# A graph network on one core: destination rows centred by the matrix engine, and several small pieces of work put into other stages

## The chip, the cores and the metric

One core of a Trainium2 chip. The metric is device microseconds of one execution, and lower is better. The engines are PE (matrix), DVE (vector), ACT (scalar functions), POOL (GpSimd, which here issues the gathers and scatters by index) and SP, which only issues DMAs and clears semaphores. Each has its own instruction queue, and they meet only through semaphores.

## The reference

N = 50,000 nodes with 64 features, E = 25,000 edges sorted by destination `dst`; `src` is random. `_L0` is a graph attention network of four layers with four heads, `_L1` a convolution over edges with batch norm.

```python
h = relu(layernorm(x))
for l in range(4):                          # _L0, each edge and a loop of each node
    fs = (h @ Ws[l]).reshape(N, 4, 64)
    e = leaky_relu(el[src] + er[dst], 0.2)  # el, er: fs times attn_l, attn_r
    alpha = softmax of e over the edges that end in one node
    h = (segment_sum(alpha * fs[src], dst) + bias).sum(heads)
x = x + h + h_bias
h = relu(layernorm(x))
total = concat([h[src], h[dst], edge_attr]) @ W_full + b_full
filter, core = split(batch_norm(total), 2)
update = segment_sum(sigmoid(filter) * softplus(core), dst)
x = x + softplus(h + batch_norm(update))
```

## The kernel before

Edges lie in 196 tiles of 128, and one turn of a loop handles a group of 4 tiles (512 edges), so that each stage over edges has G = 49 turns. Since edges are sorted by destination, a segment sum is a running sum over 512 edges of a row (a scan on DVE) that a `keep` bit resets at a segment's start. `keep_row` holds these bits in DRAM.

The program is a row of stages with a barrier of all engines between them. Within a stage each engine's program is written by `pipelined(eng, stages, down, lead, slots)`: for turn i it calls each `(lag, fn)` in the order of the list, with group i − lag. The order within a turn, and so the order of the engine's queue, is that of the list; a greater lag sets a step later, and the stage runs G + lead turns. Group k's buffers are guarded by `wait_ge(signal, at(k, back=n))`. The stages and where they lie in the profiled execution, in us:

- Weights, 0 to 62.
- The first stage over edges, 62 to 568.6: POOL gathers the x rows of source and destination (L190), DVE and ACT layernorm both (`center`, `variance`, `normalize`), and PE makes projections and searches each edge's source among the destinations. The raw destination rows are stored in DRAM as `x_dst`.
- A short block of preparation, L1106 to L1173, 568.6 to 591.1. SP loads 28 pieces of `keep_row` (L1125). DVE turns the search's results into the row numbers `row_of_source` and `row_of_x1` (L1137 to L1151, 128 x 196 elements each), then makes the gate tables `keep`, `stop`, `open_f`, `reach`, `carry_in` out of the bits (L1154 to L1166, two scans of 896 among them). PE fetches four columns (L1173).
- Four layers, each of `softmax_weights`, `messages` and (but for the last) `spread`. A layer ends with `clear_signals`, a block of its own in which SP clears each semaphore in turn (L135).
- The last stage over edges, 2319.3 to 2641.6, groups in falling order, with LEAD = 8. Per group: POOL gathers x1 of the sources out of the message table (L1229). PE spreads the layer's result (L1269), DVE ends and scans it (L1313, L1320), ACT adds a constant (L1396, `h_full`), and PE transposes `h_full` into rows (`to_edges`, L1276). DVE centres the source rows (`center`: L1337 the sum, L1338 the subtraction), adds the destination's raw rows `x_again` to PE's rows (L1343, writing x1 into `edge`), and centres those too (L1346, L1348). Then ACT squares, DVE sums (L1353) and normalizes (L1358), PE transposes `norm` (L1283) and the edge attributes (L1291), multiplies both with the convolution's weights (L1297, L1298), and DVE takes the batch statistics (`bn_stats`, L1365).
- The conv stage, 2643.9 to 2953.7: ACT computes softplus and sigmoid (`norm1` L1505 and L1506, `exponential` L1511, `logarithm` L1515, `sigmoid` L1520), DVE multiplies (`message`, L1545), scans, ends and counts, PE transposes the sums into rows (`to_rows`), ACT copies them (`take_updates`, L1526), SP fetches x1 out of `edge` beside them (`load_x1`, L1472), and POOL scatters the rows to their nodes (L1488).
- The output over all nodes, 2955.4 to 3186.6, which begins with a memset of 128 x 8192 on DVE (L1687) that SP's loads wait for (L1640).

## Time and profile before

| | us |
|---|---|
| median of 3 runs | 3179.8 (3177.26 to 3186.66) |
| the profiled execution, its own time | 3188.4 |
| its span in the trace | 3186.6 |
| PE busy, of the span | 2305.1 (72%) |
| DVE busy | 2230.3 (70%) |
| POOL busy | 1434.1 (45%) |
| ACT busy | 1248.8 (39%) |

The shares are averages over stages with different limits, and none of them tells alone what the kernel is bound by: that is read stage by stage. Times in the rows below are us from the start of the span. A row such as `x4` with one duration is a run of like instructions, from the first start to the last end. An f32 matmul is recorded as two.

### The profile page before, as it was taken

The numbers are of one execution on the slowest core, as the hardware profiler recorded it, in microseconds if no ns is written. First come the engines' busy times: TensorE is split into PE (matmuls) and PEld (weight loads), VectorE is DVE, ScalarE is ACT, GpSimd is POOL, SyncE is SP. The second block draws the span as 40 slices with busy tenths as digits, with TensorE's granted clock in tenths as the row PEclk, the third lists the DMA queues.
The fourth block names the chain that finished last, engine by engine and source line by source line (L and its number), as shares of the span: only waits on it lengthen the run. The fifth ranks groups of instructions, "written<-read, shape, count | busy, mean of one in ns | idle before, by whom it ended". The sixth has DMA issues, their size and how long they took to land. (4 is left out here: it accounts for less than half of the span.)

```text
span 3186.6 us, 38276 instructions
## 1 busy us (share of the span) xinstructions
PE 2305.1 (72%) x10796; PEld 1490.8 (47%) x10796; DVE 2230.3 (70%) x3891; ACT 1248.8 (39%) x2599; POOL 1434.1 (45%) x1389
## 2 busy tenths in 40 slices
PE   1998888399899399898569898749967781110575
PEld 1766665255575255566345565425533330000564
DVE  4766665677776567687377687468889976664698
ACT  0332332144332144343134333124445547662586
POOL 5777775000577300377500177700067754777000
PEclk9999999999855599777589877569989975555898
DMA  2333333011453111254101155202233321222464
GB/s 60 105 102 101 100 96 84 13 47 46 105 125 87 16 37 46 70 143 113 25 23 46 52 133 134 41 20 79 79 74 71 73 55 35 65 72 64 146 199 141
DMA packets 310382, 248.80 MB, mean 78 GB/s; under 512 B 149840, under 2 KB 258639, under 8 KB 310154
## 3 DMA queue, kind: packets, MB, share of 16 engines
q1 hardware_dynamic: 266270, 197.56, 20.6%
q0 software_dynamic: 43904, 48.80, 8.7%
q8 instruction: 90, 1.47, 0.2%
q14 instruction: 118, 0.97, 0.1%
HBM read 125.76 MB, written 118.06 MB: 77 GB/s over the span
## 5 line engine op out<-in xcount | busy, mean ns | idle before, releaser
L933 POOL DMA_INDIRECT edge<-table,row_of_source x588 | 596.9, 1015 | 909.4 <-POOLq L753 731.2
L871 PE MATMUL banks<-scaled_t,w_heads 128*64 128x512 f32 x784 | 380.1, 607 | 0.0
L815 DVE TENSOR_TENSOR_SCAN wide<-keep,wide,banks 64x512 f32<-64x512 uint8 x196 | 249.5, 1273 | 185.9 <-issue 161.3
L1229 POOL DMA_INDIRECT edge<-table,row_of_x x196 | 226.3, 1155 | 305.9 <-POOLq L131 244.6
L849 ACT ACTIVATE ring<-wide 128x512 f32<-128x512 f32 x196 | 123.6, 630 | 425.4 <-DVE wide L815 425.4
L1073 ACT ACTIVATE wide<-h_new 64x512 f32<-64x512 f32 x147 | 92.6, 630 | 474.1 <-DVE h_new L1019 474.1
L981 PEld LDWEIGHTS banks<-w_edge_full,wide 128*128 128x128 f32 x1176 | 219.6, 278 | 122.7 <-issue 105.9
L1488 POOL DMA_INDIRECT node_rows<-rows_conv,scatter_row x196 | 218.9, 1117 | 118.8 <-ACT rows_conv L1526 68.2
L981 PE MATMUL banks<-w_edge_full,wide 128*128 128x72 f32 x1176 | 227.7, 360 | 54.9 <-DVE self_logit L1029 54.0
L878 PEld LDWEIGHTS banks<-w_row,ring 128*128 128x128 f32 x1568 | 190.4, 191 | 161.1 <-issue 149.3
L974 PE MATMUL banks<-wide,w_row 128*64 128x512 f32 x294 | 241.6, 920 | 19.4 <-DVEq L1006 10.1
L808 DVE TENSOR_TENSOR scaled<-edge,alpha 128x1024 f32<-128x1024 f32 x196 | 236.7, 1209 | 3.7 <-PE banks L863 3.7
L190 POOL DMA_INDIRECT edge<-in_x_dram,src_row x196 | 194.5, 992 | 81.7 <-issue 58.2
L190 POOL DMA_INDIRECT got<-in_x_dram,dst_row x196 | 194.5, 992 | 59.7 <-issue 59.7
L878 PE MATMUL banks<-w_row,ring 128*128 128x68 f32 (+1 forms) x1568 | 217.9, 282 | 4.7 <-ACT ring L849 4.7
L863 PE MATMUL banks<-ident,scaled 128*128 128x128 f32 x1568 | 210.4, 279 | 11.8 <-DVE scaled L808 11.8
L1602 PE MATMUL banks<-ident,last_sum 64*128 64x64 f32 x196 | 32.2, 318 | 248.3 <-ACT rows_conv L1526 192.7
L587 PE MATMUL banks<-w_chain,norm_t 64*128 64x204 f32 x392 | 204.7, 624 | 2.5 <-ACT self_logit L565 2.5
L863 PEld LDWEIGHTS banks<-ident,scaled 128*128 128x128 f32 x1568 | 184.0, 150 | 16.7 <-DVE scaled L808 13.3
L1019 DVE TENSOR_TENSOR_SCAN h_new<-keep_next,h_new,ended 64x512 f32<-64x512 uint8 x147 | 187.1, 1273 | 1.8
L996 PE MATMUL banks<-w_node,n_norm_t 65*128 65x64 f32 x784 | 136.9, 332 | 37.7 <-ACT n_norm_t L1089 37.7
L871 PEld LDWEIGHTS banks<-scaled_t,w_heads 128*64 128x64 f32 x784 | 91.7, 137 | 148.6 <-issue 148.3
(300 smaller groups left out, 4571.9 us busy)
## 6 DMA issues: line engine op xcount, KB each, us to landing
node_rows<-x_out SPq DMA_DIRECT2D x97, 256.0 KB, 2.6
wide<-node_rows SPq DMA_DIRECT2D x48, 512.0 KB, 3.6
table<-chain_rows SPq DMA_DIRECT2D x147, 136.0 KB, 2.2
table<-rows SPq DMA_DIRECT2D x147, 136.0 KB, 2.3
nodes<-in_x_dram SPq DMA_DIRECT2D x97, 128.0 KB, 2.5
table<-x_out SPq DMA_DIRECT2D x97, 128.0 KB, 2.4
out_dram<-n_soft SPq DMA_DIRECT2D x48, 256.0 KB, 2.1
sources<-src_pad SPq DMA_DIRECT2D x49, 196.0 KB
```

The lines of the kernel that those rows point to most:

```text
L190: pool.indirect_dma_start(out=to, out_offset=None, in_=x, in_offset=bass.IndirectOffsetOnAxis(ap=rows[:, tile:tile + 1], axis=0),).then_in ...
L587: t_.matmul(bank[4 + t // 2][:, (t % 2) * width:(t % 2 + 1) * width], mine[0:D], w_chain[:].rearrange("p l w -> p (l w)"), start=True, sto ...
L808: v.tensor_tensor(scaled[:, s], edge[:, tiles, 0:D].unsqueeze(2).broadcast_to([P, TPG, H, D]), inner(alpha[:, tiles], [P, TPG, H, D]), ALU ...
L815: v.tensor_tensor_scan(out=wide[0:D, bass.ds(g * GE + 1, GE)], data0=keep[:, s], data1=bank[2 + s][0:D], initial=wide[0:D, bass.ds(g * GE, ...
L863: last = t_.transpose(bank[6 * s + pair][:, t * P:(t + 1) * P], scaled[:, s, t, 2 * pair:2 * pair + 2].rearrange("p h f -> p (h f)"), iden ...
L871: last = t_.matmul(bank[2 + s][0:D], w_heads[:, l, pair], scaled_t[:, s, pair], start=pair == 0, stop=pair == 1)
L878: last = t_.matmul(bank[4 + s][:, t * width:(t + 1) * width], ring[:, s, t * P:(t + 1) * P], w_row[:, l, 0:width], start=True, stop=True)
L933: pool.indirect_dma_start(out=edge[:, at_tile], out_offset=None, in_=tables[l], in_offset=bass.IndirectOffsetOnAxis(ap=row_of_source[:, at ...
L974: t_.matmul(bank[s % 2][0:D], w_row[:, l, 0:D], wide[:, bass.ds(g * GE + 1, GE)], start=True, stop=True).then_inc(through, 1)
L981: last = t_.matmul(bank[2 + s % 2][:, t * EDGE_W:(t + 1) * EDGE_W], here, w_edge_full[:, l + 1], start=True, stop=True)
L1229: pool.indirect_dma_start(out=edge[:, tile, 0:D], out_offset=None, in_=tables[l], in_offset=bass.IndirectOffsetOnAxis(ap=row_of_x1[:, tile ...
L1488: pool.indirect_dma_start(out=node_rows, out_offset=bass.IndirectOffsetOnAxis(ap=scatter_row[:, tile:tile + 1], axis=0), in_=rows[:, s, t] ...
```

## The change

- **The last stage.** The first stage also stores the *centred* destination rows, as `x_mid` (`save_mid`). In the last stage PE adds them up itself: it multiplies `x_mid`'s rows (256 columns) with the identity, and each tile of `h_full` with `center_of` = identity − 1/64 in place of the transpose, all into one bank. ACT copies that bank into `norm` (`take_mid`, new), and DVE's L1343, L1346 and L1348 are gone. The four transposes of the attributes become two of 128 x 128, and the product with `attr_t` becomes two of 256 columns each, with weights padded by zeros.
- **The conv stage.** `x1` comes from the message table in DRAM. The lags shrink, `lead` goes from 7 to 3, and ACT's `take_updates` is the last step of its turn.
- **The block of preparation is gone.** The 28 loads and the gate tables move into turns 2 to 34 of the first stage. The row numbers (17 instructions) go to POOL, in `messages` of layer 0.
- **Clears.** The block of `clear_signals` becomes a list of retired semaphores, which SP clears inside the next `softmax_weights`. After the last stage and the conv stage nothing is cleared.
- In `softmax_weights` the memset of `chain` (L656) now stands behind the wait for ACT's logits. The memset of the output stage is gone.

```diff
@@ first stage @@
+                def save_mid(k, g, s, turn):
+                    sp.wait_ge(centered, at(k))
+                    sp.sem_inc(sp_paced, 1)
+                    sp.dma_start(x_mid.rearrange("p (t f) -> p t f", f=D)[:, bass.ds(k * TPG, TPG)], norm[:, s % 2, :, 1]).then_inc(mid_saved[s % 2], 16)
...
+                def load_gates(k, g, s, turn):
+                    if 0 <= k - LOADS_FROM < CH:
+                        c = k - LOADS_FROM
+                        sp.dma_start(keep_u[c * H:(c + 1) * H], lanes(keep_row[c * CE:(c + 1) * CE + 1], H)).then_inc(gates_in, 16)
...
-                pipelined(sp, ((1, save_x), (4, save), (0, load)), slots=SLOTS)
+                pipelined(sp, ((0, load_gates), (2, save_mid), (1, save_x), (4, save), (0, load)), slots=SLOTS)
...
+                    v.wait_ge(mid_saved[h], 16 * (k // 2 + 1))
...
-                pipelined(v, ((3, normalize), (2, variance), (2, look_up), (1, center), (1, reach)), slots=SLOTS)
+                pipelined(v, ((3, normalize), (2, variance), (2, look_up), (1, center), (1, mark_reached), (1, gate_tables)), slots=SLOTS)
@@ softmax_weights @@
+                @block.sync
+                def _(sp):
+                    clear_retired(sp)
...
+                    v.wait_ge(logit_ready, 4)
                     for n, start in enumerate((-BIG, 0.0)):
                         link(v.memset(chain[:, n], start))
-                    v.wait_ge(logit_ready, 4)
@@ last stage, PE @@
                 def to_edges(k, g, s, turn):
+                    t_.wait_ge(x_in[s], turn * 16 + 16)
+                    t_.wait_ge(mid_taken, at(k, back=1))
+                    t_.sem_inc(pe_paced, 1)
+                    t_.matmul(bank[2][:, 0:TPG * D], ident[:], x_again[:, s].rearrange("p t f -> p (t f)"), start=True, stop=False)
                     t_.wait_ge(full_ready, at(k))
-                    t_.wait_ge(x_used, at(k, back=1))
-                    t_.sem_inc(pe_paced, 1)
                     for t in range(TPG):
-                        last = t_.transpose(bank[2][:, t * D:(t + 1) * D], h_full[:, s, t * P:(t + 1) * P], ident[0:D, 0:D])
+                        last = t_.matmul(bank[2][:, t * D:(t + 1) * D], h_full[:, s, t * P:(t + 1) * P], center_of[:], start=False, stop=t == TPG - 1)
                     last.then_inc(full_t, 1)
...
-                    t_.matmul(bank[5 + s][:], w_conv3[:], attr_t[:], start=False, stop=True).then_inc(conv_ready, 1)
+                    for b in range(2):
+                        last = t_.matmul(bank[5 + s].rearrange("p (a b q) -> p b a q", b=2, q=P)[:, b], w_conv3[:, b], attr_t[:],
+                                         start=False, stop=b == 1)
+                    last.then_inc(conv_ready, 1)
@@ last stage, SP, DVE and ACT @@
-                    sp.wait_ge(x_used, at(k, back=2))
+                    sp.wait_ge(full_t, at(k, back=2))
...
-                    v.tensor_tensor(here, bank[2][:, 0:TPG * D].rearrange("p (t f) -> p t f", f=D), x_again[:, s], ALU.add).then_inc(x_used, 1)
...
-                    link(v.tensor_reduce(now[:, 0, :, 1], here, AX_X, ALU.add))
...
+                def take_mid(k, g, s, turn):
+                    s_.wait_ge(full_t, at(k))
+                    s_.wait_ge(norm_in_psum, at(k, back=2))
+                    s_.activation(norm[:, s, :, 1], bank[2][:, 0:TPG * D].rearrange("p (t f) -> p t f", f=D), ACT.Copy).then_inc(mid_taken, 1)
...
-                pipelined(s_, ((1, finish), (4, rstd), (3, squares), (5, take), (6, keep_conv)), down=True, lead=LEAD)
+                pipelined(s_, ((1, finish), (4, rstd), (3, take_mid), (3, squares), (5, take), (6, keep_conv)), down=True, lead=LEAD)
@@ conv stage @@
-                    sp.dma_start(rows[:, s, :, 0:D], edge[:, bass.ds(g * TPG, TPG), 0:D]).then_inc(x1_in[s], 16)
-
-                pipelined(sp, ((1, load), (4, load_x1)), lead=7, slots=SLOTS)
+                    sp.dma_start(rows[:, s, :, 0:D],
+                                 tables[L - 1][N:N + EP].rearrange("(p t) w -> p t w", p=P)[:, bass.ds(g * TPG, TPG)]).then_inc(x1_in[s], 16)
+
+                pipelined(sp, ((0, load), (0, load_x1)), lead=3, slots=SLOTS)
...
-                pipelined(s_, ((1, exponential), (2, logarithm), (3, sigmoid), (0, norm1), (6, take_updates)), lead=7, slots=SLOTS)
+                pipelined(s_, ((0, norm1), (1, sigmoid), (0, exponential), (0, logarithm), (2, take_updates)), lead=3, slots=SLOTS)
...
-                pipelined(v, ((5, end), (4, message), (2, larger), (4, scan), (5, count_in)), lead=7, slots=SLOTS)
+                pipelined(v, ((1, message), (1, scan), (0, larger), (1, end), (1, count_in)), lead=3, slots=SLOTS)
...
-                pipelined(t_, ((5, to_rows),), lead=7, slots=SLOTS)
+                pipelined(t_, ((1, to_rows),), lead=3, slots=SLOTS)
@@ output stage @@
-                sp.wait_ge(nodes_cleared, 1)
...
-                v.memset(nodes[:], 0.0).then_inc(nodes_cleared, 1)
```

PE's queue in the middle of the last stage, one turn of the kernel before:

```order
L1269 MATMUL banks<-wide,w_row 64x512
L1283 MATMUL banks<-ident,norm_last 128x128 x4
L1291 MATMUL banks<-ident,attr 64x128 x4
L1297 MATMUL banks<-norm_t_last,w_conv 128x512
L1298 MATMUL banks<-attr_t,w_conv 128x512
L1276 MATMUL banks<-ident,h_full_last 128x64 x4
```

The same turn of the changed kernel:

```order
L1303 MATMUL banks<-wide,w_row 64x512
L1319 MATMUL banks<-ident,norm_last 128x128 x4
L1327 MATMUL banks<-ident,attr 128x128 x2
L1333 MATMUL banks<-norm_t_last,w_conv 128x512
L1335 MATMUL banks<-attr_t,w_conv 128x2x128 x2
L1309 MATMUL banks<-x_last,ident 128x256
L1312 MATMUL banks<-center_of,h_full_last 128x64 x4
```

Two transposes of the attributes have gone, one product of 256 columns has come, and the product with the attributes and the four small steps at the end have other forms.

ACT's queue in the middle of the conv stage, one turn of the kernel before (`arg` and `soft` at the head are `norm1`, `rows_conv` is `take_updates`, `gate` is `sigmoid`):

```order
L1505 ACTIVATE arg<-wide,bn_scale 128x512
L1506 ACTIVATE soft<-wide,bn_scale 128x512
L1526 ACTIVATE rows_conv<-banks 128x4x64
L1511 ACTIVATE soft<-soft 128x512
L1515 ACTIVATE soft<-soft 128x512
L1520 ACTIVATE gate<-soft 64x512
```

The same turn of the changed kernel:

```order
L1533 ACTIVATE arg<-wide,bn_scale 128x512
L1534 ACTIVATE soft<-wide,bn_scale 128x512
L1548 ACTIVATE gate<-soft 64x512
L1539 ACTIVATE soft<-soft 128x512
L1543 ACTIVATE soft<-soft 128x512
L1554 ACTIVATE rows_conv<-banks 128x4x64
```

The copy of the rows has moved from the third place to the last, and its group is now two behind the turn's newest, where it was six behind.

## Rows read from the trace of the kernel before

**Rows 1.** Windows: stretch, length, busy us of PE, PEld, DVE, ACT, POOL, PEclk, DMA
```profile
625.00:817.00 192.00, 187.38 (x980) 110.31 (x980) 134.29 (x148) 80.00 (x148) 0.00 (x0) 0.99 0.13 45
2400.00:2500.00 100.00, 79.11 (x307) 35.07 (x306) 95.03 (x168) 55.42 (x119) 77.75 (x68) 0.95 0.33 73
2608.00:2644.00 36.00, 23.70 (x47) 9.53 (x46) 11.57 (x23) 9.85 (x22) 0.00 (x0) 0.50 0.03 7
```

**Rows 2.** Last stage, POOL's gathers: count with shortest/median/longest ns, first and last start
```profile
L1229 POOL DMA_INDIRECT edge<-table,row_of_x x196: 940/1120/1581, 2320.0 to 2606.7; - x196
```

**Rows 3.** Last stage, timeline of one turn, DVE and POOL; columns: start, duration
```profile
2455.00 1.28 DVE L1320 TENSOR_TENSOR_SCAN h_new_last<-keep_last,h_new_last,ended_last 64x512 f32<-64x512 uint8 x1
...
2455.55 1.49 POOL L1229 DMA_INDIRECT edge<-table,row_of_x  x1 [0.30 <-issue]
...
2457.68 0.42 DVE L1343 TENSOR_TENSOR edge<-banks,x_last 128x256 f32<-128x256 f32 x1
...
2459.04 0.69 DVE L1365 BATCH_NORM_STATS2 conv_stat<-banks 128x6 f32<-128x512 f32 x1
```

**Rows 4.** PE in that turn of the last stage, and one row of `messages`
```profile
2454.95 0.63 PE L1283 MATMUL banks<-ident,norm_last 128*128 128x128 f32 x4 [1.26 <-ACT attr_t L1414]
...
2455.85 1.02 PE L1297 MATMUL banks<-norm_t_last,w_conv 128*128 128x512 f32 x2
...
2456.80 1.12 PE L1298 MATMUL banks<-attr_t,w_conv 64*128 64x512 f32 x2
...
2458.20 0.43 PE L1276 MATMUL banks<-ident,h_full_last 64*128 64x64 f32 x4 [0.28 <-issue]
...
2458.56 1.07 PE L1269 MATMUL banks<-wide,w_row 128*64 128x512 f32 x2
...
811.80 1.11 PE L878 MATMUL banks<-w_row,ring 128*128 128x68 f32 x8
```

**Rows 5.** Conv stage, POOL's scatters as a group, columns as in rows 2
```profile
L1488 POOL DMA_INDIRECT node_rows<-rows_conv,scatter_row x196: 980/984/1638, 2666.1 to 2944.3; - x196
```

**Rows 6.** Conv stage, timeline: ACT at its start; later a DVE product and a scatter
```profile
2656.70 0.81 ACT L1505 ACTIVATE arg<-wide,bn_scale 128x512 f32<-128x512 f32 x1
...
2660.08 0.81 ACT L1505 ACTIVATE arg<-wide,bn_scale 128x512 f32<-128x512 f32 x1
...
2664.89 0.36 ACT L1526 ACTIVATE rows_conv<-banks 128x256 f32<-128x256 f32 x1
...
2804.27 0.69 DVE L1545 TENSOR_TENSOR gate<-gate,soft 64x512 f32<-64x512 f32 x1
2804.32 1.49 POOL L1488 DMA_INDIRECT node_rows<-rows_conv,scatter_row  x1 [0.30 <-issue]
```

**Rows 7.** First stage, one group of POOL's gathers in the page: busy, mean ns | idle
```profile
L190 POOL DMA_INDIRECT edge<-in_x_dram,src_row x196 | 194.5, 992 | 81.7 <-issue 58.2
```

**Rows 8.** The block of preparation and the start of layer 0, timeline
```profile
568.58 9.99 SPq L1125 DMA_DIRECT2D keep_u<-keep_row  x28
...
571.01 0.36 DVE L1149 TENSOR_TENSOR tmp<-tmp 128x196 f32<-128x196 f32 x1
...
580.89 2.02 DVE L1157 TENSOR_TENSOR_SCAN open_f<-keep_u 112x896 f32<-112x896 uint8 x1
...
591.12 1.28 ACT L709 ACT_TABLE_LOAD   x1 [25.69 <-PEq L131]
...
593.83 0.62 DVE L656 MEMSET chain<- 1x240 f32 x2
...
596.47 2.03 DVE L662 TENSOR_TENSOR_SCAN fwd<-gates,logit 112x896 f32<-112x896 bf16 x1 [2.02 <-ACT logit L714]
```

**Rows 9.** All clears of semaphores by SP, then those of 1078 to 1090 us
```profile
L135 SPq EVENT_SEMAPHORE_RANGE_CLEAR  x310: 25/25/49, 588.6 to 2955.2; - x155
...
L135 SPq EVENT_SEMAPHORE_RANGE_CLEAR  x61: 25/25/25, 1083.1 to 1086.4; - x61
```

**Rows 10.** Waits of SP's queue: total us, times, longest
```profile
SPq L1640 <- DVE wide L1687: 9.1, 1, 9.1
```

More of the change, by code:

```diff
@@ L127, in pool_dma_sem, with retire_signals, clear_retired, release_retired @@
         return nc.alloc_semaphore(name=name)
-    def clear_signals():
-        with nc.Block() as block:
-            @block.sync
-            def _(sp):
-                for signal in signals:
-                    sp.sem_clear(signal)
-        for signal in signals:
+    retired = []
+    def retire_signals():
+        retired.extend(signals)
+        signals.clear()
+    def clear_retired(sp):
+        for signal in retired:
+            sp.sem_clear(signal)
+    def release_retired():
+        for signal in retired:
             nc.release_semaphore(signal)
-        signals.clear()
-    marks = {}
+        retired.clear()
     with top:
@@ L420, in build @@
             assert SLOTS == X_SLOTS
+            keep_u = mem(st, "keep_u8", [Q, CE + 1], U8)
+            open_f = wide[0:Q, 44 * GE + 1:44 * GE + 1 + 2 * CE].rearrange("p (n c) -> p n c", n=2)
+            gates_in = sem(st, "gates_in")
+            gate_own = sem(st, "gate_own")
+            low_t = sem(st, "low_t")
             x_saved = [sem(st, f"x_saved{s}") for s in range(SLOTS)]
+            mid_saved = [sem(st, f"mid_saved{n}") for n in range(2)]
             sources_in = sem(st, "sources_in")
@@ L601, in search, with gate_ends @@
                     last.then_inc(searched, 1)
-                pipelined(t_, ((3, transposes), (4, edges), (1, search)), slots=SLOTS)
+                def gate_ends(k, g, s, turn):
+                    if k == LOW_OUT_AT:
+                        t_.wait_ge(gate_own, LOW_READY)
+                        for n in range(2):
+                            t_.matmul(bank[n + 1][0:1, 0:Q], open_f[:, n, (CE - 1, 0)[n]:(CE, 1)[n]], by_head, start=True, stop=True).then_inc(low_t, 1)
+                pipelined(t_, ((3, transposes), (4, edges), (1, search), (1, gate_ends)), slots=SLOTS)
         got_mem.close()
-        by_head = ident[0:Q, 0:Q].rearrange("p (s h) -> p h s", h=H)
         def softmax_weights(l, alpha):
@@ L773, in messages, with _, link @@
                 sp_paced = sem(st, f"sp_paced_{l}")
+                if l == 0:
+                    known, row, delta = equal_to, not_above, tiles_before
+                    above = own_row = mem(st, "own_row", [P, TILES])
+                    numbered = sem(st, "numbered")
                 block = st.enter_context(nc.Block())
                 last_step = l == L - 1
+                if l == 0:
+                    @block.gpsimd
+                    def _(pool):
+                        count = [0]
+                        def link(ins):
+                            count[0] += 1
+                            ins.then_inc(numbered, 1)
+                            pool.wait_ge(numbered, count[0])
+                        link(pool.iota(row_of_source[:], pattern=[[1, TILES]], base=0, channel_multiplier=TILES))
+                        link(pool.tensor_scalar(known[:], equal_to[:], 0.0, None, ALU.is_gt))
+                        link(pool.tensor_scalar(above[:], not_above[:], 1.0, float(P * TILES - 1), ALU.is_equal, ALU.mult))
+                        link(pool.tensor_scalar(row[:], not_above[:], -2.0, float(TILES), ALU.add, ALU.mult))
+                        link(pool.tensor_tensor(row[:], row[:], tiles_before[:], ALU.add))
+                        link(pool.tensor_tensor(row[:], row[:], above[:], ALU.add))
+                        link(pool.tensor_copy(own_row[:], row_of_source[:]))
+                        for first, other, to in ((EP, own_row, row_of_source), (N, src_f, row_of_x1)):
+                            link(pool.tensor_scalar(delta[:], row[:], float(first), None, ALU.add))
+                            link(pool.tensor_tensor(delta[:], delta[:], other[:], ALU.subtract))
+                            link(pool.tensor_tensor(delta[:], delta[:], known[:], ALU.mult))
+                            link(pool.tensor_tensor(delta[:], delta[:], other[:], ALU.add))
+                            link(pool.tensor_copy(to[:], delta[:]))
                 @block.sync
@@ L1289, in transposes @@
                         t_.sem_inc(pe_paced, 1)
-                    for t in range(TPG):
-                        last = t_.transpose(bank[3][0:D, t * P:(t + 1) * P], attr[:, s, t], ident[:])
+                    for a in range(2):
+                        last = t_.transpose(bank[3][:, a * P:(a + 1) * P], attr[:, s, 2 * a:2 * a + 2].rearrange("p t f -> p (t f)"), ident[:])
                     last.then_inc(attr_in_psum, 1)
```

159 lines of the change are left out of this document (63 added, 96 removed).

## The prediction

> **What bounds the kernel now.** The chain that ended last covers only the output stage, so I went by stages: first the timeline for where each begins and ends, then busy time by windows, then single turns.
>
> The last stage is bound by DVE: in 100 us of its middle DVE is busy for 95, PE for 79 and POOL for 78 [rows 1]. POOL's 196 gathers start between 2320.0 and 2606.7, which is 286.7/48.75 = 5.88 us per group of four [rows 2]. In `messages` of layer 0 PE is busy for 187 of 192 us, DVE for 134 and POOL for nothing [rows 1].
>
> The conv stage is bound by POOL. Its 196 scatters start between 2666.1 and 2944.3 [rows 5], 1.43 us apart, 5.71 per group. The shortest takes 0.98, and the gap between two is 0.30 [rows 5, 6], so a group without any hold would take 4 x 1.28 = 5.13. The rest is scatters like the one of 1.49 us, which starts 0.05 after a DVE product with both inputs in SBUF, and lasts longer than its 0.69 [rows 6]. The gathers of the last stage show the same: 0.94 at best [rows 2], 1.49 when one starts inside DVE's scan [rows 3].
>
> In the first stage POOL sets the pace too: one of its two groups of gathers is busy for 194.5 us with a mean of 0.992, near the floor [rows 7]. The block of preparation runs from 568.6 until ACT's first instruction of layer 0 at 591.1, and nothing lies beside it [rows 8].
>
> **The change, part by part.** The sum is made against the profiled execution (its own time 3188.4, 1.8 beyond its span); the median of the runs shown, 3179.8, lies 8.6 below it, and I take that off at the end.
>
> Block of preparation: it goes as a whole, 591.1 − 568.6 = **−22.5** [rows 8]. It held the first block of clears too.
> - Its 28 loads take SP 9.99 us in the first stage [rows 8], 0.36 each, one in each turn of over 10 us, where SP has room.
> - Its row numbers go to POOL in `messages`, where POOL is idle [rows 1]. On DVE one takes 0.36 us [rows 8]; even at five times that, 17 take 31 us, beside 192. DVE's queue is relieved of them, and the next to read them are gathers of `spread`, after a barrier. Price 0; if POOL's reads held DVE throughout, 31 us of DVE beside a slack of 58 would still be under PE.
> - Its gate tables lie in three turns of the first stage, behind DVE's other work. DVE has room, but two scans of 2.02 us with two SBUF inputs [rows 8] can hold gathers of the engine that sets the pace. A full hold of both is 4 us, the other table steps about as much again: 0 to 8, I take **+3**.
>
> In the Trainium skill, the page "SBUF — State Buffer", section "Who interferes with whom", says that a DVE instruction with two SBUF inputs contends only with a GpSimd instruction that reads SBUF, and infers that issuing a gather's descriptors is therefore untouched. The gather of 1.49 in the scan [rows 3] speaks against the inference; by the rule this term would be 0 and not 3.
>
> `save_mid` adds a wait of DVE's `normalize` on a store issued one turn before. With turns of over 10 us and loads that DVE does not wait for, I take 0. The extra load of weights at the start costs 0.4 to 0.6 us: **+0.5**.
>
> Clears: 61 of them span 3.3 us [rows 9], so 0.055 each with the queue's turn; with about 0.3 for the barrier a layer's block costs 3.6. Of the 310, 41 lay in the block of preparation by the program (counted above), 3 x 61 after the layers with a `spread`, and 86 after the last three. That is 269 x 0.055 + 6 x 0.3 = **−16.6**. What hides them is SP's idleness in `softmax_weights` (SP has no other work there, and that block takes over 30 us). Without this cover they would all come back.
>
> The memset of `chain` took 0.62 in the shade of ACT: the scan behind it still waited 2.02 for the logits [rows 8]. Now it stands behind that wait: 4 x 0.62 = **+2.5**.
>
> Last stage, DVE: what goes is the stretch from L1343 to the batch statistics, 2459.04 − 2457.68 = 1.36 [rows 3]; DVE then needs 5.9 − 1.4 = 4.5. PE becomes busier. From start to start one product of 512 columns takes 2456.80 − 2455.85 = 0.95 [rows 4]. Per group then: transposes of `norm` 0.46 and two of the attributes 0.22 (four ended 0.63 after the first began); three products of 512 columns or their like, 2.9; `x_mid` with 256 columns 0.48; the four products with `center_of`. For these the rows give two ends: as transposes they took 0.36 (2458.20 to 2458.56), and four f32 products of 68 columns took 1.11 [rows 4], of which the next could overlap some; I take 0.95, nearer the second, being the same kind. Sum 5.0. ACT gets a copy like `rows_conv`'s, 0.36 [rows 6], on 55 of 100 [rows 1]: not the bound. POOL: at best 4 x (0.94 + 0.30) = 4.96 [rows 2, 3]; with one gather held by a scan 5.5; at today's mean 5.88. DVE's queue loses one more instruction with two SBUF inputs (L1348), which lowers the chance of a hold. I take 5.4, between floor and today's mean. 49 x (5.88 − 5.4) = 23.5, and with some drain at the stage's end (DVE's chain of a group is shorter) **−26**. Bounds: 0 and 49 x 0.88 = −43.
>
> What is late next there is POOL, with PE close behind. ACT's `squares` now stands behind `take_mid`, which waits for `to_edges` of the same group; PE issues that last in its turn, behind the convolution's products. With a lead of 8 groups there is slack.
>
> Conv stage: ACT's first turns are 2660.08 − 2656.70 = 3.38 apart, and the first copy starts at 2664.89 [rows 6], in the turn of lag 6. With lag 2 it stands four turns earlier, at most 13.5, but a turn is then bound by its chain through DVE, and I take **−10**. Then the rate: floor 5.13, now 5.71. ACT's copy behind all other work and DVE's products in one piece change which scatters meet them. I take 5.45: 49 x 0.26 = **−12**. If a second scatter in each group were held by 0.5, the period would be 6.2, +24; at the floor −28. The x1 rows come from DRAM and are asked for two turns ahead: 0.
>
> Output stage: SP's loads wait 9.1 for the memset [rows 10]: **−9.1**. Its cover is nothing, so the whole comes back.
>
> Sum: −22.5 + 3 + 0.5 − 16.6 + 2.5 − 26 − 22 − 9.1 = −90.2. 3188.4 − 90 = 3098, on the scale of the runs' median 3098 − 8.6 = **3089**.
>
> **The rivals.**
> - *The last stage stays at POOL's 5.88.* For it: DVE's scans remain, and the mean gather is slow today though DVE has no fewer. Against it: POOL has never been the bound there, and its gathers now drift against DVE's turn. 3089 + 23 = 3112. Chance 0.20.
> - *Both stages reach their floor.* Last stage 5.0 (PE), conv 5.13: 3089 − 19 − 16 = 3054. Chance 0.14.
> - *The conv stage is held more.* Message and scan now stand back to back in DVE's queue; period 6.2: 3089 + 37 = 3126. Chance 0.10.
> - *The clears show.* If the barrier of `softmax_weights` waits for SP, or the other engines meet it: 3089 + 17 = 3106. This is the change not doing what it says. Chance 0.03.
> - *A late load.* `x_mid` may be loaded only when `to_edges` two groups before is through, and PE, not DVE, now waits for it, with all its other products queued behind. 0.5 us in each turn: 3114. Chance 0.04.
> - *Slower: PE at half clock in the last stage.* The granted clock is 0.95 of 2.4 GHz in its middle and 0.50 (1.2 GHz) in its thinning end, and there a matmul takes 23.70/47 = 0.504 instead of 79.11/307 = 0.258 [rows 1]. PE's turn would be 5.0 x 1.95 = 9.8, and PE the bound. The kernel is level with before when the stage has lost what the rest gives, 64, at a turn of 5.88 + 1.3 = 7.2, so from 2.2/4.8 = 0.46 of the turns at half clock. At two thirds it would be 8.2: 3180 − 64 + 114 = 3230. Against it: PE becomes denser, from 79 to over 90 of 100. Chance 0.04.
>
> Against a part of the change speaks the Trainium skill, page "GPSIMD Engine Reference", section "Performance versus the Vector engine", which found an elementwise operation with two inputs nearly twice as slow on GpSimd. By it the row numbers would take about 12 us (an estimate, 17 x 0.36 x 2); no run here shows it yet, and it lies within the 31 us allowed above, in an idle queue.
>
> **How the numbers follow.** The main case, 3089, has 0.45 and its own range of 3075 to 3102: the hold of a scatter or gather by 0.15 us more or less per group in either stage. The range of 8 in 10 reaches from about the floor of both stages to the held conv stage: 3058 to 3128. A measurement of this kernel can tell about 0.3%, 9.5 us, from no change. All cases but the last end more than 50 us below before; the slow clock in part only gives the 0.01 of no change. Faster 0.95, same 0.01, slower 0.04.
>
> **What would show it.** Layer 0 begins where the first stage ends, within 1 us of a barrier; POOL has 17 instructions in `messages`; SP's clears lie inside `softmax_weights`; DVE in the last stage is busy for about 80 of 100, POOL and PE over 90; gathers there start 5.4 per group apart; the first scatter comes 12 us after the conv stage begins instead of 22, and they run 5.45 apart; the output stage's first load comes 9 us sooner. I would be wrong if POOL's mean time per gather rises as DVE's turn shortens, if PE waits for ACT's `take_mid`, or if the granted clock of the last stage falls.

## The result

The changed kernel takes 3108.24 us (median of 4 runs, 3100.39 to 3118.66), the kernel before 3183.23 (median of 4, 3177.26 to 3193.14). The ratio is 0.9748, 95% interval 0.9722 to 0.9774. That is 75 us between medians. The forecast was 3089, with 3075 to 3102 for its main case and 3058 to 3128 for 8 in 10: the time lies in the wide range, 6 us above the main case's. Between the two profiled executions it is 88: 3188.4 before, and 3100.39 now, the fastest of its four runs.

Each stage begins with ACT loading its tables, so the starts of those loads cut both executions into stages. All of the following compares the two profiled executions.

| stage, us | before | after | difference | forecast |
|---|---|---|---|---|
| up to the first stage | 61.9 | 61.0 | −0.9 | +0.5 |
| first stage and preparation | 529.2 | 509.4 | −19.8 | −22.5 + 3 |
| four `softmax_weights` | 140.6 | 143.1 | +2.5 | +2.5 |
| three `messages` 0 to 2 | 579.4 | 579.9 | +0.5 | 0 |
| three `spread`, with clears | 811.3 | 804.1 | −7.2 | −10.8 |
| `messages` 3, with clears | 197.0 | 193.6 | −3.4 | −1.9 |
| last stage, with clears | 324.6 | 285.7 | −38.9 | −26 − 2.1 |
| conv stage, with clears | 311.5 | 299.8 | −11.7 | −22 − 1.8 |
| output | 231.1 | 221.9 | −9.3 | −9.1 |

The sum of the differences is −88.1; the forecast's was −90.2. Rows of the table miss by up to 12 us in either direction and cancel, so that the sums agree is in part luck.

**The block of preparation and the clears.** Before layer 0 ACT now stands still for 3.15 us, where it was 25.69 [rows 8], and DVE's wait between two layers is 5.7 us. Timeline of the changed kernel, the start of `softmax_weights` in layers 0 and 1:

```profile
570.47 1.28 ACT L775 ACT_TABLE_LOAD   x1 [3.15 <-PEq L419]
...
575.81 0.62 DVE L723 MEMSET leaky<- 1x240 f32 x2 [2.62 <-ACT logit L780]
576.46 2.02 DVE L728 TENSOR_TENSOR_SCAN fwd<-gates,logit 112x896 f32<-112x896 bf16 x1
...
1062.50 0.97 DVE L715 TENSOR_TENSOR edge<-edge,const_logit 128x784 f32<-128x784 f32 x1 [5.74 <-PEq L985]
```

The wait for the logits that stood ahead of the scan, 2.02 [rows 8], now stands ahead of the memset, 2.62, and the scan follows the memset at once: 0.62 on the path in each layer. In the kernel before, DVE's wait at the place of the last row was 9.35 in layer 0 and 9.29 in layers 1 and 2; 3.6 have gone, as forecast from [rows 9].

**The gate tables in the first stage.** Timeline of the changed kernel, POOL and DVE where the two long scans run:

```profile
370.70 0.94 POOL L198 DMA_INDIRECT got<-in_x_dram,dst_row  x1 [0.30 <-issue]
370.74 2.03 DVE L574 TENSOR_TENSOR_SCAN wide<-keep_u 112x896 f32<-112x896 uint8 x1
371.94 1.57 POOL L198 DMA_INDIRECT edge<-in_x_dram,src_row  x1 [0.30 <-issue]
372.80 2.02 DVE L575 TENSOR_TENSOR_SCAN wide<-keep_u 112x896 f32<-112x896 uint8 x1
373.81 1.76 POOL L198 DMA_INDIRECT got<-in_x_dram,dst_row  x1 [0.30 <-issue]
```

This shows the hold to the tenth. The gather at 370.70 starts 0.04 before the scan and is not held. The one at 371.94 starts with 0.83 of the scan left and is held for 0.63; the one at 373.81 starts with 1.01 left and is held for 0.82. A gather is held when it starts while a DVE instruction with two SBUF inputs runs, for what is left of it less a little: 0.19 for a scan, 0.12 for an elementwise instruction (the scatter at 2663.89 below is held for 0.23 of 0.35 left). Over the last stage and the conv stage, before and after, this gives the duration of all but six of 784 gathers and scatters within 0.03 us. The two scans cost 1.4 us. Over the whole stage the mean gather went from 0.992 to 0.998, which is 2.3 us for 392 of them, in a term forecast as 3.

**The last stage.** First POOL's gathers as a group (answering [rows 2]), then busy time by windows (as in [rows 1]), both of the changed kernel:

```profile
L1262 POOL DMA_INDIRECT edge<-table,row_of_x x196: 941/947/1882, 2291.8 to 2557.2; - x196
```

```profile
2325.00:2415.00 90.00, 90.00 (x434) 57.74 (x433) 81.17 (x127) 62.70 (x144) 68.35 (x72) 1.00 0.36 86
2440.00:2540.00 100.00, 89.33 (x421) 55.05 (x419) 75.62 (x120) 57.03 (x137) 78.73 (x70) 1.00 0.32 77
```

The mean period is (2557.2 − 2291.8)/48.75 = 5.44, forecast 5.4. It is a mean of two states that last for many turns. From 2330.93 to 2395.96 thirteen groups of gathers start 5.00 apart, and PE is busy all the time. From 2449.89 to 2553.47 eighteen turns take 5.75 in the mean, 6.3 and 5.2 by turns, and PE idles for a tenth. Two pieces of the timeline, POOL and DVE's scan, the first in the one state, the second in the other:

```profile
2350.95 0.95 POOL L1262 DMA_INDIRECT edge<-table,row_of_x  x1 [0.30 <-issue]
2351.05 1.28 DVE L1359 TENSOR_TENSOR_SCAN h_new_last<-keep_last,h_new_last,ended_last 64x512 f32<-64x512 uint8 x1
2352.20 0.94 POOL L1262 DMA_INDIRECT edge<-table,row_of_x  x1 [0.30 <-issue]
...
2483.93 1.28 DVE L1359 TENSOR_TENSOR_SCAN h_new_last<-keep_last,h_new_last,ended_last 64x512 f32<-64x512 uint8 x1
...
2484.47 1.49 POOL L1262 DMA_INDIRECT edge<-table,row_of_x  x1 [0.30 <-issue]
...
2486.27 1.19 POOL L1262 DMA_INDIRECT edge<-table,row_of_x  x1 [0.30 <-issue]
```

In the fast state the gather starts 0.10 ahead of the scan, in every turn. Once something shifts the phase, the gather falls inside the scan. Between the two states lies a pause of POOL of 1.57 us ahead of the gather at 2440.24, for which the profile shows no reason; e9 (below) has one of 2.00 at 2392.34 and goes on at 5.00.

**The conv stage.** POOL's scatters as a group (answering [rows 5]) and two of the held ones with what holds them:

```profile
L1516 POOL DMA_INDIRECT node_rows<-rows_conv,scatter_row x196: 982/986/1967, 2588.8 to 2867.1; - x196
```

```profile
2663.55 0.69 DVE L1573 TENSOR_TENSOR gate<-gate,soft 64x512 f32<-64x512 f32 x1
2663.89 1.21 POOL L1516 DMA_INDIRECT node_rows<-rows_conv,scatter_row  x1 [0.30 <-issue]
...
2666.69 1.57 POOL L1516 DMA_INDIRECT node_rows<-rows_conv,scatter_row  x1 [0.30 <-issue]
```

The first starts inside DVE's `message`, the second 0.50 us into the scan that DVE began at 2666.19.

The stage begins at 2576.8, so the first scatter comes after 12.0 us where it was 22.1. But the period is (2867.1 − 2588.8)/48.75 = 5.71, to the hundredth what it was.

**POOL's instructions in `messages` of layer 0** run from 605.0 to 622.3, 17 us where the forecast estimated 12 and allowed 31, and the stage takes 193.1 where it took 193.0. The same operation twice, the first time beside a DVE product with two SBUF inputs, the second time beside a scan whose second input is in PSUM:

```profile
613.90 1.60 DVE L905 TENSOR_TENSOR scaled<-edge,alpha 128x1024 f32<-128x1024 f32 x1
...
614.50 1.46 POOL L870 TENSOR_TENSOR tiles_before<-tiles_before,equal_to 128x196 f32<-128x196 f32 x1
...
619.35 1.27 DVE L912 TENSOR_TENSOR_SCAN wide<-keep,wide,banks 64x512 f32<-64x512 uint8 x1 [1.03 <-issue]
619.64 0.60 POOL L870 TENSOR_TENSOR tiles_before<-tiles_before,equal_to 128x196 f32<-128x196 f32 x1
```

DVE's product took 1.60 there, where its mean is 1.21: here both sides lose.

### The profile page after: what moved, and what is told of

It is laid out like the page before. It is cut to its first block and busy times, and to the rows that moved or that the text cites. A ratio compares the mean times of both kernels' runs of the same rounds, so it can differ in the third digit from the quotient of the medians.

```text
span 3098.5 us, 38691 instructions
## 1 busy us (share of the span) xinstructions
PE 2303.9 (74%) x11090; PEld 1533.5 (49%) x11090; DVE 2165.0 (70%) x3732; ACT 1258.2 (41%) x2648; POOL 1434.6 (46%) x1405
## 5 line engine op out<-in xcount | busy, mean ns | idle before, releaser
L1262 POOL DMA_INDIRECT edge<-table,row_of_x x196 | 205.7, 1049 | 299.0 <-POOLq L819 238.3
L1124 DVE TENSOR_TENSOR edge<-edge,banks 128x256 f32<-128x256 f32 x147 | 59.5, 405 | 158.6 <-DMA edge<-table,row_of_source 158.4
```

Source lines behind the costliest of these rows:

```text
L1262: pool.indirect_dma_start(out=edge[:, tile, 0:D], out_offset=None, in_=tables[l], in_offset=bass.IndirectOffsetOnAxis(ap=row_of_x1[:, tile ...
```

## The experiments

The experiments fell on four chips, of two kinds by their times. On a chip of the first kind the kernel before takes 3191.5 (e9, e10), near the 3183 of the result. On three of the second kind it takes 3593 (e1 to e4), 3599 (e5 to e8) and 3603 (e11, e12), and the changed kernel itself 3563 (e5). A single instruction of DVE, ACT or POOL takes the same time on both kinds, and so do the stages without gathers: 193 us for `messages`, 222 for the output. In e5 the stages with gathers are longer than in the profile of after by 22 to 31%, the conv stage by 2%. In them engines stand still at times, for instance at these two starts of POOL and DVE in the last stage of e5 (during the second wait POOL went on to issue 18 gathers, up to 2716.38):

```profile
2776.23 0.94 POOL L1262 DMA_INDIRECT edge<-table,row_of_x  x1 [6.59 <-DVE h_new_last L1359]
```

```profile
2722.49 0.42 DVE L1368 TENSOR_REDUCE stat_last<-edge 128x4 f32<-128x256 f32 x1 [27.86 <-issue]
```

Some expectations below call this late landings. That isn't borne out: by the packet records the last packet of a gather or scatter ends 2.16 us after its start in e5 and 2.13 in the profile of after (medians over 1372). What the engines wait for in these pauses stays open. So a time is compared only within a kind, and what depends on POOL's pace is read on the first. Even there the kernels may stand on different chips (e1 to e4, e11 and e12 against e5 and e8; e9 and e10 perhaps against the result), and the kernel before itself differs between these by 4 to 8 us. A difference of that size between whole kernels decides nothing, and stages and single waits are read instead.

### The last stage undone (e1, e10)

The changed kernel with the last stage of before; the first stage still stores the centred rows.

```diff
-                    t_.matmul(bank[2][:, 0:TPG * D], ident[:], x_again[:, s].rearrange("p t f -> p (t f)"), start=True, stop=False)
...
-                        last = t_.matmul(bank[2][:, t * D:(t + 1) * D], h_full[:, s, t * P:(t + 1) * P], center_of[:], start=False, stop=t == TPG - 1)
+                        last = t_.transpose(bank[2][:, t * D:(t + 1) * D], h_full[:, s, t * P:(t + 1) * P], ident[0:D, 0:D])
...
+                    v.tensor_tensor(here, bank[2][:, 0:TPG * D].rearrange("p (t f) -> p t f", f=D), x_again[:, s], ALU.add).then_inc(x_used, 1)
```

> The changed kernel with the last stage of before (DVE adds and centres the destination rows again, transposes and products as before); the first stage still stores the centred rows. Theory A (the last stage's edit gave what the profile of after shows there): the stage takes about 285.6 + 37 = 322 us again and the kernel is 37 us slower than the changed one, near 3145; its gathers start 5.9 us apart per group and PE's granted clock falls to 0.5 as they end. Rival B (what the stage won came from what lies before it, such as the state in which the clock enters): under 300 us, and the kernel within 15 of the changed one.

> The same kernel as e1, again, for a chip where before takes about 3180. Theory A: the last stage takes 322 us again (285.6 with the edit), with the clock at 0.5 in its last 38 us, and the kernel 37 us more than the changed one. Rival B: under 300 us. On a chip like the second the stage is bound by landings, and 367 comes again.

On the second kind (e1) the kernel takes 3545.31 and the stage 367.4, against 3562.91 and 374.1 in e5: the edit wins nothing there. On the first (e10) the kernel takes 3137.85, 29.6 more than the changed kernel's 3108.24 (27 by the ratios to the kernel before on each chip), and the stage 314.7 against 285.7. Neither expectation's number: the edit is worth 29 us and not 37. The gathers and the tail of the stage in e10, by group and by windows:

```profile
L1257 POOL DMA_INDIRECT edge<-table,row_of_x x196: 940/1122/1587, 2296.6 to 2583.8; - x196
```

```profile
2582.00:2611.00 29.00, 17.87 (x50) 7.48 (x48) 13.07 (x27) 10.06 (x22) 2.16 (x3) 0.79 0.06 13
```

The period is (2583.8 − 2296.6)/48.75 = 5.89, the same as before the change. From the last gather to the stage's end it takes 27 us in e10, with a granted clock of 0.79; in the profile of before it took 35 (without the clears) at 0.50 [rows 1, 2], and in that of after 20. So of the 37 us between the two profiles (without clears), 8 are a tail in which the clock was lower with the same instructions; of the 29 that the edit gives, (5.89 − 5.44) x 48.75 = 22 lie in the period, 7 in the tail.

### The conv stage's order undone (e2, e12)

```diff
-                pipelined(s_, ((0, norm1), (1, sigmoid), (0, exponential), (0, logarithm), (2, take_updates)), lead=3, slots=SLOTS)
+                pipelined(s_, ((1, exponential), (2, logarithm), (3, sigmoid), (0, norm1), (6, take_updates)), lead=7, slots=SLOTS)
```

and the same for DVE, PE and SP.

> The changed kernel with the conv stage's lags and lead of before (copy of rows third in ACT's turn), x1 still from the message table. Theory A (the new order only moves the first scatter ahead, POOL's rate is the same): first scatter 22 us after the stage begins instead of 12, period 5.71 in both, the kernel 10 us slower than the changed one. Rival B (reading x1 from the table costs rate and the order wins it back): the period rises above 5.85 and the kernel is 17 us or more slower.

> The same kernel as e2, again, for a chip where before takes about 3180. Theory A (the order moves only the first scatter): conv stage 299.8 + 10 = 310, first scatter 22 us after its beginning, mean scatter 1.12 as with the new order. Rival B (the new order also changed the rate): mean scatter 1.10 or less or 1.14 or more, the stage under 306 or over 314.

Both fell on the second kind. The stage takes 311.6 and 312.5 against 305.5 in e5, the first scatter comes 22.1 after the stage begins against 12.0, and the mean scatter is 1.116 and 1.114 against 1.095 (1.063 to 1.092 in e1, e3 and e6, which have the new order too). The kernels take 3555.7 and 3564.3 against 3562.9, which resolves nothing. The stage and its first scatter speak for A. The scatters are held less with the new order there, by 0.02 to 0.05 each, but it brings no rate: from first to last they take 280 and 281 us with the old order, 281 to 284 with the new. On the first kind the mean scatter was 1.117 with the old order and 1.116 with the new.

### The clears undone (e3, e11)

```diff
     def retire_signals():
...
+        with nc.Block() as block:
+            @block.sync
+            def _(sp):
+                for signal in signals:
+                    sp.sem_clear(signal)
...
```

and the clears inside `softmax_weights` out, with two more such blocks after the last stage and the conv stage; e11 does it to the kernel of e8.

> The changed kernel with the semaphores cleared in blocks of their own again, with barriers, after the first stage, after each layer and after the last two stages over edges. Theory A (each clear costs its 0.055 us and each block a barrier): 2.5 + 3 x 3.6 + 2.3 + 1.9 + 1.7, about 19 us slower than the changed kernel. Rival B (in the profile of after the stages with a spread of layers 1 and 2 are shorter by 1.4 us only, so the clears were half hidden or something else came in): under 12 us slower.

> The kernel of e9 (all operands in PSUM, 3016 us, stages with a spread within 0.4 us of each other) with the blocks of clears restored, so that their price is read without the gathers' changing holds. Theory A (0.055 us for each clear and 0.3 for a barrier, all of it on the path): each stage with a spread 253.6 + 3.6 = 257.2, the first stage + 2.5, the kernel 19 us above 3016. Rival B (half of it is hidden, as the profile of the changed kernel seemed to say): each such stage under 256, the kernel under 3026.

e3 takes 3565.52 (3547.99 to 3576.13), 2.6 more than e5: with a spread of 28 us among its own runs, its time says nothing. e11 takes 3597.02 (10 runs) and e8 3578.54 (8 runs): 18.5 us more, near the 19 of A, though not on the kind for which it was expected, and on another chip than e8's, where the kernel before takes 4 us more. The single waits say it better. DVE's wait ahead of layer 1, e11 and then e8, from each timeline:

```profile
1312.71 0.98 DVE L717 TENSOR_TENSOR edge<-edge,const_logit 128x784 f32<-128x784 f32 x1 [4.44 <-PEq L134]
```

```profile
1306.72 0.98 DVE L715 TENSOR_TENSOR edge<-edge,const_logit 128x784 f32<-128x784 f32 x1 [0.32 <-PEq L985]
```

The block is seen to cost 4.1 here, and 3.6 on the first kind. Taken at each block of e11 in the same way, by how long the engine that ended last had been done when the next stage began, against e8, the six cost 3.1, 4.1, 3.9, 3.6, 3.6 and 2.2: 20 us in all. Those of e3 against e5 agree to the tenth. So nothing of a block is hidden, and rival B falls. As a whole the blocks were not put back on the first kind.

### The operands in PSUM (e4, e6, e7, e8, e9)

These take away what holds POOL: the work is the same, but steps that had two SBUF inputs get one from PSUM. In the conv stage (e4; e7 has the first line alone):

```diff
-            gate = mem(st, "gate", [P, 2, GE])
+            gate = banks[:, 4:6]
...
-            arg = mem(st, "arg", [P, SLOTS, GE])
+            arg = banks[:, 0:2]
+            sums = banks[0:D, 6:8]
...
-                    v.tensor_tensor_scan(out=wide[0:D, bass.ds(g * GE + 1, GE)], data0=keep[:, s], data1=gate[0:D, s % 2],
+                    v.tensor_tensor_scan(out=sums[:, s % 2], data0=keep[:, s], data1=gate[0:D, s % 2],
```

`end` reads the sums from PSUM too, and with two slots for `arg` ACT's `norm1` also waits for `larger` of two groups before. In the last stage (e6), and all but the last change also in the stages with a spread (e8 and e9, which hold all of it):

```diff
-                    t_.wait_ge(ended_ready, at(k, back=2))
+                    t_.wait_ge(spread_out, at(k, back=2))
...
-                    v.scalar_tensor_tensor(out=ended[:, s], in0=keep[:, s], scalar=0.0, in1=bank[s][0:D],
+                    v.scalar_tensor_tensor(out=bank[s][0:D], in0=keep[:, s], scalar=0.0, in1=bank[s][0:D],
...
-                    v.tensor_tensor_scan(out=h_new[:, s, ::-1], data0=keep[:, s, ::-1], data1=ended[:, s, ::-1],
+                    v.tensor_tensor_scan(out=h_new[:, s, ::-1], data0=keep[:, s, ::-1], data1=bank[s][0:D, ::-1],
...
-                    total = stat[:, s].rearrange("p n (t e) -> p n t e", e=2)[:, 0, :, 0]
+                    total = bank[7][:, s * TPG:(s + 1) * TPG]
```

> The changed kernel with arg, gate and the running sums of the conv stage in PSUM, so that none of DVE's four elementwise steps there has two SBUF inputs; the work is the same. Theory A (scatters are held for as long as a DVE instruction with two SBUF inputs runs at their start): all 196 scatters take 0.98 to 0.99, the period falls from 5.71 to 5.15, the stage by 27 us. Rival B (the scatters are slow by their own DMA, or by any DVE work): mean stays near 1.1 and the stage within 5 us of 300.

On the second kind no scatter is held any more; group of e4's scatters:

```profile
L1517 POOL DMA_INDIRECT node_rows<-rows_conv,scatter_row x196: 982/985/1017, 3029.6 to 3310.4; - x196
```

but the stage takes 302.1 against 305.5 in e5, since ten gaps ahead of scatters, up to 5.2 us and together 29 above the usual 0.3, have come in, where e5 has 11 us of such gaps. They eat 18 of the 22 us of holds. On the holds A is right and B falls; on the time neither is.

> The changed kernel itself, as the yardstick for the kernels beside it, since the first four experiments fell on a chip where the kernel before takes 3593 instead of 3183. Theory A (the chips differ in how soon transfers land, and the change is worth the same on both where no transfer is waited for): on a chip like the first 3108, on one like the second about 3545. Rival B (the last stage's gain is lost when transfers land late): 3560 or more on the second.

e5 takes 3562.91 where the kernel before takes 3598.84: ratio 0.9884, interval 0.9838 to 0.9929. The change is worth 36 us there instead of 75, and by e1 the last stage is no shorter with the edit. B's time came, without its reason.

> The changed kernel with DVE's ended rows and the sum of the source rows of the last stage in PSUM, so that the scan and the subtraction have one SBUF input each; the work is the same. Theory A (the stage leaves its turn of 5.0 us for one of 5.77 when gathers meet DVE instructions with two SBUF inputs): holds of gathers only by the normalization, mean under 0.98, period 5.0 to 5.1, the stage 15 to 22 us shorter than with the changed kernel. Rival B (the longer turn comes from PE or ACT, and the holds only fill it): the stage within 5 us. Where transfers land late the stage is bound by them, and both expect no difference.

> The changed kernel with only the gate of the conv stage in PSUM: message and scan have one SBUF input each, the other two steps still two. In the changed kernel scatters were held 9.7 us in all by the message and 15.4 by the scan, and by nothing else. Theory A (holds by whatever has two SBUF inputs at a scatter's start): the scatters move in phase and now meet the larger step and the end instead; mean between 0.99 and 1.08, stage 8 to 25 us shorter. Rival B (only a long instruction such as the scan can hold): mean 0.99, stage 25 us shorter at least.

e6 has a mean gather of 0.959, and only the normalization still holds some, as A expected of it; its stage takes 380.2 against 374.1. e7 has a mean scatter of 1.059. Of its holds 9.5 us are now by the end step (L1586), which held none in the changed kernel, and 1.0 by `larger`: they move on to what has two SBUF inputs. Its stage takes 304.4 against 305.5. The kernels take 3563.8 (e6) and 3553.48 (e7) against e5's 3562.91; the 9 us less of e7 are not clear of runs that spread over 11.

Another 4.2 us of holds in e7 the rule by the start doesn't cover. They are of 15 scatters that start in the scan, which has one SBUF input now, with `larger` (two SBUF inputs) beginning 0.5 to 1.0 us later, for instance:

```profile
3214.12 1.28 DVE L1579 TENSOR_TENSOR_SCAN wide<-keep_conv,wide,banks 64x512 f32<-64x512 uint8 x1 [0.73 <-DVE banks L1573]
3214.28 1.42 POOL L1516 DMA_INDIRECT node_rows<-rows_conv,scatter_row  x1 [0.30 <-DMA node_rows<-rows_conv,scatter_row]
...
3215.32 0.66 DVE L1569 SCALAR_TENSOR_TENSOR soft<-arg,soft 128x512 f32<-128x512 f32 x1
```

So a scatter can also be held in its course. What decides it was not tried further.

> The changed kernel with the operands of e4 and e6 and also the ended rows of the three stages with a spread in PSUM. Theory A (the holds are the price of POOL's stages): 27 us less in the conv stage, 15 to 22 less in the last, and in each stage with a spread the mean gather falls from 1.02 to about 0.96, 4 x 0.06 x 49 = 12 us: in all about 80 us under the changed kernel where gathers set the pace. Rival B (a stage with a spread waits for landings, not for POOL): nothing there, in all 45.

> The same kernel as e8, again, since e5 to e8 ran on a chip where transfers land so late that the gathers' holds lie in their shade. On a chip where before takes about 3180: theory A (the holds are the price of POOL's stages) conv stage 299.8 - 27 = 273 us, last stage 285.6 less 15 to 22, each stage with a spread 270 less 8 to 12, the kernel near 3030. Rival B (scatters and gathers are then bound by their landing at once): less than half of it, over 3070. On a chip like the second: no difference from the changed kernel again.

e8, on the same chip as e5, takes 3578.54, 15.6 more than e5, against both expectations, though its holds are gone as well (mean gather 0.957, mean scatter 0.985). Its last stage takes 387.2 against 374.1. What costs there wasn't tried further. In it PE may write a bank only when the scan has read it, which shortens PE's lead; whether that is the cause is not shown. e9, the same kernel on the first kind, takes **3016.17** (3014.83 to 3018.44), ratio 0.9453 to before (0.9436 to 0.947), 92 us below the changed kernel (94 by the ratios to the kernel before on each chip). POOL's three groups in its page, then its last stage and conv stage by windows:

```profile
L1030 POOL DMA_INDIRECT edge<-table,row_of_source x588 | 557.0, 947 | 832.1 <-POOLq L819 653.8
...
L1262 POOL DMA_INDIRECT edge<-table,row_of_x x196 | 185.6, 947 | 300.5 <-POOLq L819 239.4
...
L1517 POOL DMA_INDIRECT node_rows<-rows_conv,scatter_row x196 | 192.6, 983 | 93.0 <-issue 53.5
```

```profile
2300.00:2400.00 100.00, 100.00 (x482) 64.21 (x481) 89.93 (x141) 69.52 (x161) 74.29 (x79) 1.00 0.38 86
2580.00:2680.00 100.00, 12.52 (x76) 9.50 (x76) 72.45 (x96) 67.92 (x114) 75.27 (x77) 0.50 0.27 74
```

| stage, us | after | e9 | expected of e9 |
|---|---|---|---|
| three `spread` | 264.4, 269.9, 269.8 | 253.5, 253.2, 253.9 | 8 to 12 less each |
| last stage | 285.7 | 267.7 | 15 to 22 less |
| conv stage | 299.8 | 273.8 | 27 less |

The conv stage's 26 us are the holds alone: 196 x (1.116 − 0.983). Two of the three stages with a spread gave more than expected, 17 and 16 us.

A scan no longer holds a scatter that starts inside it, and it is the same with gathers. Timeline of e9:

```profile
2600.22 0.98 POOL L1517 DMA_INDIRECT node_rows<-rows_conv,scatter_row  x1 [0.30 <-issue]
...
2605.03 1.28 DVE L1582 TENSOR_TENSOR_SCAN banks<-keep_conv,banks 64x512 f32<-64x512 uint8 x1 [0.77 <-DVE banks L1575]
2605.37 0.98 POOL L1517 DMA_INDIRECT node_rows<-rows_conv,scatter_row  x1 [0.30 <-issue]
```

## Why the prediction was right, step by step

**Right, with its size.** The block of preparation and the gate tables (−19.5, measured −19.8), the memset of `chain` (+2.5), the output's memset (−9.1, measured −9.3), the row numbers on POOL at nothing, and the clears: the blocks cost what was forecast (3.6 seen in DVE's wait between layers, 20 over the six blocks of e11). The three stages with a spread gave only 7.2 instead of 10.8, because their gathers took longer to issue in this execution: 260.5 and 260.3 us from first to last in layers 1 and 2, where it had been 258.3. Their mean went from 1.020 and 1.019 to 1.031 and 1.030, so it is holds again, as nothing in the change touches these stages' loops.

**The last stage: mechanism right, two things off.** PE's turn of 5.0 is seen for thirteen turns and throughout e9. The four products with `center_of` took 1.10 from start to end, so the row of `messages` had been the right one to go by. The period came out at 5.44, but not as a turn with half a hold: it is a mean over two states, 5.00 and 5.75. The tail was forecast at −2.5 and was worth about −7, and in the profile of before it held another 8 us of low clock. I had read the 0.50 in that window [rows 1] only as a danger for the change.

**The conv stage: the step on the rate failed.** "ACT's copy behind all other work and DVE's products in one piece change which scatters meet them. I take 5.45": it stayed 5.71. What meets what did change. In the kernel before, of 196 scatters 37 were held by the message (18.7 us in all), 9 by the scan (4.9) and 17 by the larger step (2.4); in the changed kernel 46 are held by the message (9.8) and 38 by the scan (16.1). The sums are both 26. The counts show that the phase is nearly locked, about one scatter of each group of four meeting the same instruction; that the two orders must catch the same share doesn't follow, and on the second kind they didn't. The term was −12, measured 0: the forecast put the new order between the floor and today's rate without a reason why it should hold less. The other term of this stage, the first scatter 10 us earlier, was right.

**The rivals.** The last stage at today's mean was half true, in its second half. The floor in both stages isn't reached by this change, but e9 reaches it: 5.0 and 5.18 = (2780.6 − 2528.1)/48.75, near the 5.13 of an unheld group. The rival of a conv stage held more came in its condition, scan and message back to back with 48 scatters starting in the scan, but the period is 5.71 and not 6.2. The late load fell: between 2300 and 2556 PE waits 4.9 us in all ahead of the product with `x_mid`, 0.5 at most. The clears fell, and so did the slow clock in the last stage: it is 1.00 in the middle now. One sign was put wrong: POOL was to be busy for over 90 of 100 there. It is for 76 and 79, since by the forecast's own rows 0.94 of busy time and 0.30 of gap allow no more than 76 without holds. By the Trainium skill, "SBUF — State Buffer", section "Who interferes with whom", a DVE instruction with two SBUF inputs contends with one of GpSimd's that reads SBUF; e9 bears it out. The same section's inference that descriptors for gathers are not stopped by it is contradicted by every hold above, and by e9, whose gathers lose their holds when the second SBUF input goes. The gathers here take their row numbers from a tile in SBUF (`row_of_x1`), so the rule itself may cover them; which of POOL's accesses is held is not shown.

**The time, 19 us above the forecast.** Only 2 of these come from the terms, and that is so because 11 us too little in the last stage and 12 too much in the conv stage cancel, which is luck. The other 17 are scale. The forecast took 8.6 off because the profile of before lay that far above its median; the profile of after is the fastest of its runs and lies 7.8 below its own. The runs of the kernels with holds spread over 10 to 18 us on the first kind (before, after, e10), those of e9 over 3.6. That the holds' phase makes this spread is not shown: on the second kind e8, without holds, spreads over 22.

## What to carry to other kernels

When POOL issues gathers or scatters and sets the pace, look in the timeline at what DVE runs at their starts. If it has two SBUF inputs, put one in PSUM: this took 92 us off 3108 here on one chip (and on another, where other pauses rule, it cost 16), where reordering the same instructions took nothing off the rate. When one engine's pace triggers another's work, the two can stay in one phase for many turns, and a mean duration can be a mixture of two states; read single turns before taking a value between them.

## What the runs showed of the hardware

- A gather or scatter by index is held if it starts while a DVE instruction with two SBUF inputs runs, for the rest of that instruction less 0.19 us for a scan (0.63 of 0.83, 0.82 of 1.01 left) and 0.12 for an elementwise one. One that starts 0.04 or 0.10 earlier than the instruction isn't. In e7 15 scatters were held (4.2 us in all) that started outside such an instruction, 0.5 to 1.0 us ahead of one.
- Elementwise instructions of POOL are held likewise: 0.60 free, 1.46 held, for the same operation.
- Chips of two kinds ran the same kernel in 3183 to 3192 us and in 3593 to 3603. Instructions of DVE, ACT and POOL took the same time on both, and the packets of gathers ended equally soon (2.13 and 2.16 us after the start); the second had pauses of up to 28 us in the stages with gathers, whose cause stays open. The change was worth half as much there.
- A block in which SP clears 61 semaphores cost 3.6 us on the path between two layers (DVE's wait 9.3 with it, 5.7 without).
